# Splitting one interleaved group of attention score products on PE, with the output projection between its two parts

## The reference

```
q = split_heads(layernorm(x) @ Wq.T + bq)      # 32 x 16 heads x 128 x 8
k, v = split_heads(ctx @ Wk.T + bk), split_heads(ctx @ Wv.T + bv)
scores = einsum('bhqd,bhkd->bhqk', q, k) / sqrt(8)
scores = where(mask == 0, -1e9, scores)
p = softmax(scores)
x = x + (einsum('bhqk,bhkd->bhqd', p, v) joined over heads) @ Wo.T + bo
```

## Time and profile before

| | |
|---|---|
| median of 3 runs | 358.33 us (357.87 to 359.38) |
| the profiled execution, its own time | 358.66 us |
| its span, first to last instruction | 356.9 us |
| mean granted TensorE clock | 0.952 |
| PE busy | 300.5 us, 84% of the span |
| DVE busy | 280.2 us, 79% |
| ACT busy | 256.1 us, 72% |
| POOL busy | 178.7 us, 50% |

### The profile page before, as it was taken

The page is one execution under the profiler, slowest core; times in us unless marked ns, Lnnn a source line. Parts: engine busy times, 40 slices in busy tenths (PEclk is TensorE's granted clock), DMA queues, the critical chain, the costliest instruction groups (busy, mean ns, idle before and its releaser), DMA issues.

```text
span 356.9 us, 9561 instructions
## 1 busy us (share of the span) xinstructions
PE 300.5 (84%) x3621; PEld 197.6 (55%) x3621; DVE 280.2 (79%) x590; ACT 256.1 (72%) x457; POOL 178.7 (50%) x322
## 2 busy tenths in 40 slices
PE   2789999998689999999999999779986668670996
PEld 1577877776256666666666667534332223220996
DVE  5359988866867888988989885857869997898563
ACT  3268788886357888888888888558787766993850
POOL 3468999993422355766566573200047774663000
PEclk9989999999858999999999999989999999896799
DMA  5781666564661000000000000000000000000124
GB/s 143 249 259 32 191 188 214 181 216 141 201 193 47 5 5 2 4 5 3 4 2 5 5 3 2 2 0 0 2 0 0 1 0 0 1 0 0 31 88 119
DMA packets 23751, 22.67 MB, mean 64 GB/s; under 512 B 3545, under 2 KB 21402, under 8 KB 23578
## 3 DMA queue, kind: packets, MB, share of 16 engines
q1 hardware_dynamic: 22170, 21.78, 19.7%
q10 hardware_dynamic: 1536, 0.28, 0.4%
HBM read 15.75 MB, written 6.31 MB: 62 GB/s over the span
## 4 chain that ended last, share of the span: by engine, by line
PE 40%; DVE 28%; POOL 12%; issue 7%; ACT 6%; DMA 5%; SPq 2%; POOLq 0%; DVEq 0%; ACTq 0%
DVE nm L1347 10%; DVE mxs L1554 10%; PE banks L881 7%; PE banks L841 6%; PE banks L613 6%; PE banks L655 6%; PE banks L677 4%; POOL rstd L352 3%; PE banks L622 3%; PE banks L673 3%; POOL pickd L371 3%; DMA k_dram<-klo 2%; DVE G L1612 2%; DMA X3T<-m_dram 2%; PE banks L537 1%
## 5 line engine op out<-in xcount | busy, mean ns | idle before, releaser
L1347 DVE TENSOR_REDUCE nm<-banks 128x8 f32<-128x1024 f32 x64 | 78.3, 1224 | 16.6 <-PE banks L613 13.2
L1039 ACT ACTIVATE PT<-banks,bmask,vmask 128x1024 f32<-128x1024 f32 x64 | 76.9, 1201 | 3.9 <-PE banks L622 2.1
L841 PE MATMUL banks<-X3T,upT 128*128 128x512 f32 x96 | 45.6, 620 | 14.1 <-DVE mxs L1554 9.4
L484 POOL TENSOR_TENSOR G<-ng,sq 128x1536 int32<-128x1536 int32 (+3 forms) x10 | 27.9, 2789 | 40.0 <-DVE sq L1579 40.0
L1554 DVE TENSOR_REDUCE mxs<-G 128x1 f32<-128x1536 int32 (+5 forms) x29 | 41.9, 1467 | 6.8 <-ACT G L1080 6.8
L655 PE MATMUL banks<-PT,VP 128*32 128x128 f32 x1024 | 42.5, 285 | 0.0
L841 PEld LDWEIGHTS banks<-X3T,upT 128*128 128x128 f32 x96 | 18.0, 197 | 39.8 <-issue 18.1
L915 ACT ACTIVATE h<-X,shift,rstd 128x128 f32<-128x128 f32 x64 | 26.4, 482 | 14.3 <-POOL shift L397 14.3
L613 PE MATMUL banks<-kd,qd 32*128 32x128 f16 x512 | 26.4, 222 | 5.7 <-DVE nm L1347 1.9
L655 PEld LDWEIGHTS banks<-PT,VP 128*32 128x32 f32 x1024 | 24.7, 111 | 9.1 <-issue 3.7
L433 POOL CAST NM<-nm 128x64 bf16<-128x64 f32 x32 | 7.6, 236 | 41.7 <-DVE nm L1347 41.7
(11 more groups left out here) (182 smaller groups left out, 698.1 us busy)
## 6 DMA issues: line engine op xcount, KB each, us to landing
kd<-k_dram SPq DMA_DIRECT2D x32, 128.0 KB, 2.7
qd<-q_dram SPq DMA_DIRECT2D x32, 128.0 KB, 2.6
ctxg<-in_ctx_dram SPq DMA_DIRECT2D x8, 256.0 KB, 3.4
X3T<-m_dram SPq DMA_DIRECT2D x1, 1792.0 KB, 8.8
out_dram<-y SPq DMA_DIRECT2D x7, 256.0 KB, 2.2
X<-in_x_dram SPq DMA_DIRECT2D x3, 512.0 KB, 9.4
k_dram<-khi SPq DMA_DIRECT2D x8, 128.0 KB, 1.8
k_dram<-klo SPq DMA_DIRECT2D x8, 128.0 KB, 2.1
```

The source lines that it names most:

```text
L484: nc.gpsimd.tensor_tensor(GI[:, c], ng[:, u, part], sq[:, u, part], ALU.mult).then_inc(S["b_t"], 1)
L841: m = pe.matmul(bank(2 + FC * (g % 2) + k), w[:, k * P:k * P + P], grp(X3T, g), start=True, stop=True)
L1039: act.activation(PT[:, a, :], bank(2 + 2 * a, 2), ACT.Exp, bias=bmask[:, n:n + 1], scale=vmask[:, n:n + 1]).then_inc(S["t_exp"], 1)
L1347: V.tensor_reduce(nm[:, n % 2, 2 * NSET * a:2 * NSET * (a + 1)], bank(0, 2).rearrange("p (h m) -> p h m", m=P), AX.X, ALU.max, negate=True ...
```

## The change

In the second half of `cross(n)`, for n = 1 to 28, the sixteen interleaved products become two groups of eight, with `project` between them. The wait for DVE's reduction stays ahead of the first group. For n = 0 and in the first halves the interleaved order stays; for n = 29 to 31, where no query-row products are left, `project` stays where it was. No instruction is added or removed, and no DMA is touched.

```diff
+            def scores_apart(n, a):
+
+                scores_q(n + 3, 1 - a)
+                project(n - 1)
+                scores_k(n + 1, a)
+
             def scores(n, a):
...
                     pe.wait_ge(S["t_max"], 2 * n + 6 + a)
-                    scores(n, a)
+                    if n > 0 and a == 1:
+                        scores_apart(n, a)
+                    else:
+                        scores(n, a)
                 elif n + 1 < B:
                     scores_k(n + 1, a)
...
                 pe.wait_ge(S["t_exp"], 2 * n + 2)
                 pv(n, 1)
-                if n > 0:
+                if n > 0 and n + 3 >= B:
                     project(n - 1)
                 both(n, 1)
```

## The result

The changed kernel takes 363.82 us (median of 6 runs, 360.85 to 366.33), the kernel before 358.37 us on the same footing (6 runs, 357.45 to 359.38). The ratio is 1.0133, interval 1.0086 to 1.018: it is slower, by 5.45 us by the medians. The forecast was slower by 9.8 us (368.1). The direction and the place were right, the size was 1.8 times too large.

A forecast was written before the change was run, and what follows sets the result against it. The prediction took the loop to be bound by five PE steps and one DVE reduction. PE's new steps summed to 4.14 us against 3.79, times 28 sequences: 358.3 + 9.8 = 368.1 us, 8-in-10 range 361.5 to 370.0.

The forecast's parts named there:

- What bounds the loop: Five PE steps plus one DVE reduction: 1.98 us to the second score group, then 0.44 + 1.24 + 0.14, period 3.80.
- The wait that `project` used to cover: Ahead of the second half's query products PE stands still 0.24 us for DVE's first reduction, restarting 0.14 after it.
- T: The start of `scores(n, 0)`, the first group of score products, on PE; the forecast's times count from it.
- `queries` and `max_rows`: PE steps ahead of `pv`, taken as 0.09 + 0.37 us; the low end took 0.06 + 0.32.
- The split: Two groups of eight products take twice the time of one interleaved group of sixteen: about 0.23 us more on PE.
- The crossing of forms: A group of eight ahead of a whole-array instruction takes 0.32 us, not 0.23; applied to query products ahead of `project`.
- `project` and ACT's copy: `project` still costs 0.42 us; ACT's copy of its result waits 0.3 us, its effect on `pv` hidden by 0.4.
- The sum: PE's steps over one sequence add to a 4.14 us period, 0.35 longer, 9.8 us over 28 sequences.
- the low end of the sum: Query group at 0.23 and 0.06 + 0.32 from `max_rows` to `pv`: period 3.97, 0.18 longer, 5.0 us in all.
- DVE's reductions: First rival: both reductions on DVE are the loop, period 3.62 us, 4.8 us faster at 353.5; chance 0.11.
- The clock: Rival: with more idle time PE is granted 1.2 GHz in part of the loop, well over 370 us; chance 0.03.
- the second rival: No change: `project` and the key products overlap on PE, its part near 1.99 us; 358.3 within 1.8; chance 0.09.

The follow-up runs named there:

- experiment 9: Kernel before, with the first half's key products moved ahead of their wait and its query products alone behind it: ratio 0.9986 to the kernel before, period 3.790 us.
- experiment 8: Changed kernel with `project` and the key products exchanged, so query and key products are neighbours behind the wait: ratio 1.0024 to the kernel before, period 3.787 us.
- experiment 4: Changed kernel with the sixteen products interleaved again behind the wait, then added maxima, and `project` last: ratio 1.0033 to the kernel before, period 3.800 us.
- experiment 1: Changed kernel with `project` back ahead of the wait, eight query then eight key products behind it: ratio 1.000 to the kernel before, period 3.788 us.
- experiment 3: Changed kernel with the second half's key products moved ahead of the wait: ratio 0.9982 to the kernel before, period 3.755 us where the granted clock is 1.00.
- experiment 7: Changed kernel with row maxima over only the first 64 of each head's 128 scores: ratio 0.9914 to the kernel before, period 3.756 us.
- experiment 6: Changed kernel with key products ahead of the wait in both halves and `project` last: ratio 0.9893 to the kernel before, period 3.667 us.
- experiment 5: Changed kernel with the second half's key products ahead of the wait and `project` last: 353.11 us against 357.68 for the kernel before, ratio 0.9862.
- experiment 2: Changed kernel with all sixteen products interleaved behind the wait, then `project`, then added maxima: ratio 0.9944 to the kernel before.

## Why the prediction was right or wrong

*What bounds the loop.* Nearly right. The path ran through one reduction and five steps on PE as said, but from the reduction it reached `turn` through DVE's `attend` and not through the first group (experiment 9). I had written some 0.08 us of waiting at `turn` down as slack of PE and still counted it in the 1.98. This changed nothing in the sum, which had the wait removed.

*The wait that `project` used to cover.* Right in kind, too dear. I took 0.14 us from the end of a reduction to PE's restart, off the first groups, and so put the query products at T + 1.80. They came at T + 1.72, for ahead of the second group the restart takes 0.06 (162.84 to 162.90 in the changed kernel, and the same in experiment 8). **This term was the largest error: 0.08 us of each sequence, 2.2 us in all.** What the group holds is not the reason, since the sixteen interleaved products of experiment 4 restart as soon (163.05 to 163.10). The rows rather go by the number of waits in the program: the first group stands behind two waits in a row (`t_mTc`, then `t_max`), the second behind one. Experiment 9 put the key products between the two, and the restart fell to 0.06 in the first half as well. `pv` in experiment 4 stands behind two waits too and starts 0.14 after ACT's copy (164.46 to 164.60), where `queries`, behind one, starts 0.06 after its own (160.85 to 160.91 in the kernel before). No run took a wait away, so this reason is likely and not proven. The kernel before had shown a short restart behind a single wait, at a granted clock of 0.50, in rows that I did not read:

```profile
99.22 1.22 DVE L1347 TENSOR_REDUCE nm<-banks 128x8 f32<-128x1024 f32 x1
...
100.49 0.60 PE L613 MATMUL banks<-kd,qd 32*128 32x128 f16 x8 [0.63 <-DVE nm L1347]
```

99.22 + 1.22 = 100.44, and PE starts at 100.49.

*`queries` and `max_rows`.* I chose 0.09 + 0.37 from the steady loop over 0.06 + 0.32 from its end. Measured 0.07 + 0.32. In the steady loop before, `queries` was waiting for ACT's copy, which this row of the kernel before shows ending at 160.85, 0.06 ahead of `queries` at 160.91. In the changed kernel PE comes later than ACT (the copy ends 0.58 us ahead), and the dearer form goes away. The other runs agree: in experiments 1 and 9 the copy ends 0.05 us ahead and `pv` follows `queries` by 0.37, in experiments 3, 7 and 8 it ends over 0.3 us ahead and `pv` follows by 0.32. No run changed this copy alone, so why a `queries` that waited takes longer is open. 0.07 us per sequence, 2.0 us in all: the second term that was mis-sized.

```profile
160.48 0.37 ACT L1018 ACTIVATE oun<-banks 128x256 f32<-128x256 f32 x1
```

and in the changed kernel, where `queries` starts at 164.27

```profile
163.32 0.37 ACT L1027 ACTIVATE oun<-banks 128x256 f32<-128x256 f32 x1
```

*The split.* The number was right: 0.33 and 0.23 measured for 0.32 and 0.24. The reason given, that two groups of eight take twice the time of one of sixteen, was wrong as a rule: it named the split as the cost. Experiments 1, 6 and 8 show that two neighbouring groups on different rows overlap without being interleaved in the program. What costs is `project` between them, an instruction on the whole array: 0.33 + 0.23 against 0.35. It was partly luck that the number came out all the same: the change happened to put just such an instruction between the groups.

*The crossing of forms.* 0.33 ahead of `project`, as taken. With experiment 4 it can be seen from the other side too: `project` takes 0.42 us ahead of score products and 0.32 ahead of `max_rows`, which also uses the whole array. The Trainium skill's rule of a drain (TensorEngine Tiling (Array Packing), Key Properties) agrees with both, at about 0.1 us a crossing.

*`project` and ACT's copy.* Right: the copy moved and nothing waited for it in the changed kernel. It is the next bound when `project` moves further back (0.18 us in experiment 4).

*The sum.* Predicted 1.80 + 0.32 + 0.42 + 0.24 + 0.32 + 0.09 + 0.37 + 0.58 = 4.14. Measured 1.72 + 0.33 + 0.42 + 0.23 + 0.32 + 0.07 + 0.32 + 0.57 = 3.98. The steps came in the order that was forecast, and the loss of 0.35 us was 0.19. The step that failed is the pricing of two terms: the restart behind DVE's reduction (0.14 taken, 0.06 measured, so 1.80 was 1.72) and `max_rows` with `queries` (0.09 + 0.37 taken, 0.07 + 0.32 measured). Together they are 0.15 of the 0.16 us. Both were read off rows with waits around them that the changed second half, or what follows it, does not have. The measured 0.19 is close to the low end of the sum, 0.18, but that end got there with a cheaper query group (0.23, measured 0.33) and kept the dear restart: this agreement is luck. I should have asked of each row whether its wait would still be there in the new order.

*The rivals.* DVE's reductions do not bound (experiment 7: each is 0.54 us shorter and the period falls by 0.22, the idle time alone). The clock did not fall: it is 1.00 from 120 to 200 us of the changed kernel's profile. The rule that I cited from the Trainium skill beside the second rival (TensorE: Matmul & The Clock Gate, Part 3), that matmuls start strictly in order, does not hold here. In experiment 1 the first key products start at 164.74, ahead of query products at 164.78 that precede them in the program. That rival's mechanism, key products slipping in beside others, exists; `project` between them keeps it from happening in the changed kernel.

## What to carry to other kernels

In these runs, products of small contraction on different rows of the array overlap when they are neighbours in the program, interleaved by hand or not. So keep such groups together, with no instruction on the whole array between them, and move ahead of a wait what does not need it. Here key products ahead of the wait and `project` behind the added maxima gave 1.4% where the change lost 1.3%. When a cost is taken from a row of the old order, first look whether that row contains a wait which the new order removes.

## What the runs showed of the hardware

**Matmuls out of program order.** Groups on different row positions start alternately though issued one group after the other (experiments 1, 5, 6, 8).

**A clock that does not rise while PE is full.** In the profiled executions of experiments 2 and 3 the loop ran for long at 1.2 GHz, a granted clock of 0.50. In experiment 2 this lasted from 96 to 284 us of the span, with PE busy all through windows like this one; a sequence takes 5.98 us there. In experiment 3 it rose to 1.00 near 212 us, in a loop that had been as full before (50.00 us busy of 50 from 150 to 200). In the other nine profiled executions it rose between 103 and 112 us. What decides it is open.

```profile
215.00:225.00 10.00, 10.00 (x157) 5.92 (x145) 5.48 (x10) 5.58 (x10) 5.08 (x12) 0.50 0.01 2
```
